# Spacing the routing scatters of two stages over their turns, with four row buffers and loops of four turns

## What is computed

```python
x = x + L0_gnn(layernorm(x), adj)      # 17-tap convolution, messages, GRU gates
x = x + L0_ffn(layernorm(x))           # top 2 of 16 experts
...
# inside the last feed-forward layer
x = x + y @ wo.T                       # causal attention of 4 heads
flat = rmsnorm(x, ln2)
probs = softmax(flat @ router_w.T); tp, ti = top_k(probs, 2)
return x + sum_e weight_e * expert_e(flat)
```

## Time and profile before

| | |
|---|---|
| median of 3 runs | 3343.19 us (3338.99 to 3350.63) |
| the profiled execution | 3378.2 us |
| its span, first to last instruction | 3376.4 us |
| mean granted TensorE clock over the span | 0.904 |
| busy share of the span: PE, PEld, DVE, ACT, POOL | 80%, 63%, 65%, 52%, 26% |
| scatters of routed rows (line 756) | 320, 315.9 us busy |

### The profile page before, as it was taken

The page is one execution under the profiler, slowest core; times in us unless marked ns, Lnnn a source line. Parts: engine busy times, 40 slices in busy tenths (PEclk is TensorE's granted clock), DMA queues, the critical chain, the costliest instruction groups (busy, mean ns, idle before and its releaser), DMA issues. The chain is left out here.

```text
span 3376.4 us, 67489 instructions
## 1 busy us (share of the span) xinstructions
PE 2714.6 (80%) x19706; PEld 2131.5 (63%) x19706; DVE 2205.6 (65%) x6555; ACT 1742.1 (52%) x5034; POOL 872.7 (26%) x863
## 2 busy tenths in 40 slices
PE   5798995888677586578999998899987777669992
PEld 4566674877457585265777877566654444468882
DVE  5666664444467554767888885699986667644445
ACT  2233332444456453475656563677756666445553
POOL 0222332444425343230001010000001343434332
PEclk9899997999789798889999999899998888779996
DMA  5111111222332121320000000000010000022115
GB/s 195 42 46 48 57 45 47 67 63 65 117 123 76 50 58 47 126 79 1 1 1 0 0 1 10 26 19 25 19 34 37 21 24 20 26 59 56 53 53 165
DMA packets 142589, 169.06 MB, mean 50 GB/s; under 512 B 19920, under 2 KB 118224, under 8 KB 141776
## 3 DMA queue, kind: packets, MB, share of 16 engines
q1 hardware_dynamic: 116688, 118.67, 11.9%
q0 software_dynamic: 21504, 44.74, 3.9%
q10 hardware_dynamic: 4224, 3.59, 0.4%
HBM read 115.87 MB, written 51.05 MB: 49 GB/s over the span
## 5 line engine op out<-in xcount | busy, mean ns | idle before, releaser
L1375 PE MATMUL bank<-ffn_e_xT,ffn_e_mine 128*128 128x128 f32 x3360 | 462.8, 285 | 56.3 <-ACT ffn_e_mine L1309 24.4
L1233 POOL DMA_INDIRECT y_rows<-ffn_e_rows_out,ffn_e_scatter_at x352 | 339.0, 963 | 523.4 <-DVE ffn_e_rows_out L1261 331.6
L1375 PEld LDWEIGHTS bank<-ffn_e_xT,ffn_e_mine 128*128 128x128 f32 x3360 | 423.1, 199 | 68.0 <-issue 41.7
L756 POOL DMA_INDIRECT sorted_rows<-ffn_rows,ffn_slot x320 | 315.9, 987 | 231.2 <-issue 220.1
L1385 PE MATMUL bank<-ffn_e_mine,ffn_e_hid 128*128 128x128 f32 x1968 | 294.9, 283 | 39.1 <-DVE ffn_e_hid L1281 17.6
L1281 DVE TENSOR_TENSOR ffn_e_hid<-ffn_e_act,bank 128x256 f32<-128x256 f32 (+1 forms) x280 | 135.9, 485 | 276.3 <-ACT ffn_e_act L1335 245.1
L1309 ACT ACTIVATE ffn_e_mine<-constants 128x512 f32 (+1 forms) x352 | 250.9, 714 | 87.1 <-issue 64.4
L1385 PEld LDWEIGHTS bank<-ffn_e_mine,ffn_e_hid 128*128 128x128 f32 x1968 | 256.2, 196 | 55.9 <-DVE ffn_e_hid L1281 26.5
L2752 ACT ACTIVATE gnn_prob<-bank,gnn_low 128x256 f32<-128x256 f32 x512 | 203.0, 500 | 107.0 <-DVE gnn_low L2666 107.0
L1335 ACT ACTIVATE ffn_e_act<-bank 128x256 f32<-128x256 f32 (+1 forms) x280 | 120.8, 431 | 247.0 <-PE bank L1375 174.1
L1269 DVE TENSOR_SCALAR ffn_e_mine<-constants 128x256 f32 (+2 forms) x352 | 123.6, 354 | 119.6 <-PE bank L1385 73.0
(11 more groups left out here) (515 smaller groups left out, 6552.1 us busy)
## 6 DMA issues: line engine op xcount, KB each, us to landing
g_adj<-in_adjT SPq DMA_DIRECT2D x48, 512.0 KB, 3.8
ffn_e_rows_in<-sorted_rows SPq DMA_DIRECT2D x346, 66.0 KB
ffn_c_y<-y_rows SPq DMA_DIRECT2D x80, 256.0 KB, 3.7
g_adj_rows<-in_adj SPq DMA_DIRECT2D x16, 512.0 KB
gnn_adj<-in_adjT SPq DMA_DIRECT2D x16, 512.0 KB, 3.8
constants<-in_ffn SPq DMA_DIRECT2D x1, 6281.0 KB, 22.1
y_rows<-ffn_e_rows_out,ffn_e_scatter_at POOLq DMA_INDIRECT x352
constants<-in_ffn SPq DMA_DIRECT2D x1, 5204.0 KB, 15.5
```

What stands on the lines that cost most here:

```text
L756: eng.indirect_dma_start(c.sorted_rows, bass.IndirectOffsetOnAxis(r.slot[par][:, k, j:j + 1], 0), r.rows[par][:, j, :], None).then_inc(r.d ...
L1233: g.indirect_dma_start(c.y_rows, bass.IndirectOffsetOnAxis(scatter_at[par][:, k:k + 1], 0), rows_out[par][:, k, :], None).then_inc(scatter ...
L1375: ins = pe.matmul(chunk(part, ch), chunk(weights[:, i * HALF:(i + 1) * HALF], ch), x, start=True, stop=True)
```

## The change

1. **Scatters in eight pieces.** `dispatch` takes a set `mine` of the eight scatters. The new `Route.pool_few` issues those. Ahead of each piece it waits for its own last addition (`paced`) and adds one column of a scratch tile.
2. **gnn0.** GpSimd's turn t scatters the rows of t-2 one at a time, each after a semaphore of TensorE of the same turn. Three of them stand ahead of the root of t-1, which was first before.
3. **att3.** GpSimd's turn t computes the root and the addition first, as before, then scatters 6 and 7 of turn t-3 and 0 to 5 of turn t-2, each (but the first of a group) after one of ScalarE's exponentials.
4. **Buffers.** `ROUTE_DEPTH` is 4 for ffn0 and ffn3; every route call gets a buffer number modulo 4.
5. **Loops.** gnn0 uses `by_fours`: turns 0 to 3 written out, 4 to 11 in a loop of four bodies, 12 to 15 written out. att3 uses the new `staggered_fours` with `STAGES = (2, 3, 8, 4)`: -2 to 7 written out, 8 to 11 in a loop that runs once, 12 to 18 written out.
6. Two semaphores that only ffn1 uses are no longer made for the others, and the last scatters of gnn0 (turn 14 after the loop, turn 15 in the table stage) stay in one piece.

```diff
+def staggered_fours(eng, body, ahead, behind, begin, left):
+    for t in range(-ahead, begin):
+        body(t, t % 4)
+    with eng.Fori(begin, TURNS - left - 3, 4) as t:
+        for i in range(4):
+            body(t + i, i)
+    for t in range(TURNS - left, TURNS + behind):
+        body(t, t % 4)
...
-                def turn(t, par, first, last):
+                def turn(t, four, first, last):
+                    par, one, two = four % 2, (four + 3) % 4, (four + 2) % 4
                     if first:
                         return
+                    if isinstance(t, int) and t == 1:
+                        g.wait_ge(route.zeroed, 2)
+                        route.pool_rstd(g, 0)
+                        return
+                    route.pool_few(g, t - 2, two, (0,))
+                    g.wait_ge(ghn_ps, t + 1)
+                    route.pool_few(g, t - 2, two, (1,))
+                    g.wait_ge(dist_ps, t + 1)
+                    route.pool_few(g, t - 2, two, (2,))
                     route.pool_rstd(g, t - 1)
-                    if not (isinstance(t, int) and t == 1):
-                        route.pool_dispatch(g, t - 2, par)
-                every_turn(g, turn)
+                    g.wait_ge(c2_ps, t + 1)
+                    route.pool_few(g, t - 2, two, (3,))
+                    g.wait_ge(nmp_ps, t + 1)
+                    route.pool_few(g, t - 2, two, (4,))
+                    g.wait_ge(route.logits_ps, t)
+                    route.pool_few(g, t - 2, two, (5,))
+                    g.wait_ge(r_ps, t + 1)
+                    route.pool_few(g, t - 2, two, (6,))
+                    g.wait_ge(z_ps, t + 1)
+                    route.pool_few(g, t - 2, two, (7,))
+                by_fours(g, turn)
                 route.pool_rstd(g, TURNS - 1)
-                route.pool_dispatch(g, TURNS - 2, 0)
+                route.pool_dispatch(g, TURNS - 2, 2)
...
-ROUTE_DEPTH = {"ffn0": 2, "ffn1": 4, "ffn3": 2}
+ROUTE_DEPTH = {"ffn0": 4, "ffn1": 4, "ffn3": 4}
...
-def dispatch(eng, c, m, r, par):
+def dispatch(eng, c, m, r, par, mine=range(2 * TT)):
     for k in range(m.top):
         for j in range(TT):
+            if k * TT + j not in mine:
+                continue
...
+    def pool_few(self, g, t, par, mine):
+        if 0 in mine:
+            done = counted(g, t + 1)
+            g.wait_ge(self.slots_ready, done)
+            g.wait_ge(self.h_ready, done)
+        wait_past(g, self.paced, 2 * TT * t + mine[0])
+        g.tensor_tensor(self.c.tick[:, 5:6], self.c.tick[:, 0:1], self.c.tick[:, 0:1], ALU.add).then_inc(self.paced, 1)
+        dispatch(g, self.c, self.m, self.r, par, mine)
...
-    STAGES = (2, 3, 6, 4)
+    STAGES = (2, 3, 8, 4)
...
                     if on(t - 1):
                         route.pool_rstd(g, t - 1)
                         with_x1(t - 1)
+                    if on(t - 3) and not (isinstance(t, int) and t - 3 == TURNS - 1):
+                        route.pool_few(g, t - 3, (four + 1) % 4, (6,))
+                        after(g, exp_ready, t + 1, 8, 5)
+                        route.pool_few(g, t - 3, (four + 1) % 4, (7,))
                     if on(t - 2) and not (isinstance(t, int) and t - 2 == TURNS - 1):
-                        route.pool_dispatch(g, t - 2, par)
-                staggered(g, turn, *STAGES)
+                        if isinstance(t, int) and t == 2:
+                            g.wait_ge(route.zeroed, 2)
+                        route.pool_few(g, t - 2, (four + 2) % 4, (0,))
+                        for first, turns, exps in ((1, 1, 6), (2, 1, 8), (3, 2, 1), (4, 2, 3), (5, 2, 4)):
+                            after(g, exp_ready, t + turns, 8, exps)
+                            route.pool_few(g, t - 2, (four + 2) % 4, (first,))
+                staggered_fours(g, turn, *STAGES)
```

More of the change, by code:

```diff
@@ L460, in turn @@
                     if not first:
-                        route.vector_shift(v, t - 1, 1 - par, before)
+                        route.vector_shift(v, t - 1, one, before)
                     if not last:
@@ L477, in turn @@
                     if not first:
-                        route.vector_first(v, t - 1, 1 - par, before)
+                        route.vector_first(v, t - 1, one, before)
                         route.vector_second(v, t - 1, before)
@@ L547, in turn @@
                     if not first:
-                        route.scalar_rows(a, t - 1, 1 - par)
+                        route.scalar_rows(a, t - 1, one)
                     a.wait_ge(shared_ps, t + 1)
@@ L643, in turn @@
                     if not first:
-                        route.tensor_hT(pe, t - 1, 1 - par)
+                        route.tensor_hT(pe, t - 1, one)
                     if not last:
@@ L807, in __init__ @@
              "den_ready pair_sum pair_eps pair_inv rank_ps counted used_ready "
-             "picked slots_ready inside_ready kept_ready routed").split())
-        self.scattered = r.dispatched
+             "picked slots_ready routed").split())
+        self.inside_ready, self.kept_ready = (sem(n) if m.capacity else None for n in ("inside_ready", "kept_ready"))
+        self.scattered, self.paced = r.dispatched, sem("paced") if m.top > 1 else None
     def tiles_(self, ap):
@@ L3002, in with_x1, with turn @@
                     g.tensor_tensor(c.X[:, rows_, :], c.X[:, rows_, :], c.X1[:, rows_, :], ALU.add)
-                def turn(t, par):
+                def turn(t, four):
+                    par = four % 2
                     if on(t - 1):
@@ L3124, in turn @@
                         row_stats(t - 1)
-                staggered(v, turn, *STAGES)
+                staggered_fours(v, turn, *STAGES)
             @block.scalar
@@ L3205, in turn @@
                     if on(t - 2):
-                        route.scalar_rows(a, t - 2, par)
+                        route.scalar_rows(a, t - 2, (four + 2) % 4)
                     if on(t - 1):
@@ L3224, in turn @@
                         evac_T(1, 1)
-                staggered(a, turn, *STAGES)
+                staggered_fours(a, turn, *STAGES)
             @block.tensor
@@ L3339, in turn @@
                     if on(t - 2):
-                        route.tensor_hT(pe, t - 2, par)
+                        route.tensor_hT(pe, t - 2, (four + 2) % 4)
                     if on(t - 1):
```

30 lines of the change are left out of this document (15 added, 15 removed).

## The result

The changed kernel takes **3230.05 us** (median of four runs, 3227.11 to 3233.31) beside 3344.07 for the kernel before: a ratio of **0.9658**, 95% interval 0.9639 to 0.9678, or 114 us less. The forecast was 73 us less, 3270, and its range ended at 3230. The direction and both places were right; the size of one place was wrong by a factor of more than two, and a term that I had put at nothing is not nothing.

The account below looks back on a forecast made before the run. Bursts of scatters were taken to hold TensorE's news and so lengthen turns of the graph and attention stages. Spacing them saves 36 + 37 = 73 us from the 3343.2 us median, giving 3270 us, range 3230 to 3325.

Parts of the forecast that it names:

- The mechanism: Graph and attention stages: scatters following each other without a gap hold back news of TensorE's finished matmuls from waiting engines.
- rival B: Only one of the two stages gains, gaps being too short in the attention: 3290 to 3330 us, chance 0.2.
- D: Every single scatter holds TensorE's news for 2.77 us, so the kernel gets slower: 3396 us, chance 0.09.
- From about the second scatter: Where in a burst of scatters the holding of TensorE's news was said to begin.
- Until 2 to 3 us after the last: When the holding was said to end, counted from the start of a burst's last scatter.
- Rival C: Scatters are not the cause, only the norm's delay is added: 3354 us, or 3343 if hidden; chance 0.07.
- Graph stage, 36 us: Turns fall from 30.3 to 27.7 us (26.4 + 0.8 norm's delay + 0.5 residual holds), saving 2.6 in 14 turns.
- The holding is no product of the profiler as a whole: Both stages: 54 + 65 us charged to holding exceed the 35 us by which the profiled execution exceeded the median.
- Attention, 37 us: Spaced scatters leave 22.5 us of the 25.6 us turn, saving 3.1 us in each of twelve turns.
- 2.3 us: Attention: holding left per turn after spacing, about half of an upper bound of 4.2 us.
- 20.2: Attention: undisturbed turn in us, 18.73 plus VectorE's 1.07 of routing and some gaps.
- Loops by four and buffers: Both stages: no gain or loss, longer code covered by prefetch; if that failed, about 1 us per turn.

Follow-up runs that it names:

- e1: Changed kernel with the attention's scatters put back as one burst of eight, so only the graph stage is spaced: 3317.4 us, 0.9928 of before.
- e3: Changed kernel with both stages scattering in one burst of eight again, four buffers and loops by four kept: 3353.0 us, 1.0036 of before.
- e2: Changed kernel with the graph stage's scatters put back as one burst of eight, so only the attention is spaced: 3267.9 us, 0.9776 of before.
- e7: Changed kernel with all eight scatters at the old place, no waits for marks, three chained additions ahead of each: 3260.6 us, 0.9682 of before.
- e8: Changed kernel with scatters in back-to-back pairs, marks between pairs, norm first in the graph stage: 3243.1 us, 0.9636 of before.
- e5: Changed kernel with GpSimd's norm ahead of the three scatters in the graph stage, nothing else: 3246.7 us, 0.9649 of before.
- e11: Changed kernel with the graph stage back to loops by two and two row buffers, scatters still spaced: 3074.4 us, 1.0001 of before (chip C).
- e13: The kernel before, unchanged, run and profiled a second time, on chip D: 3344.1 us, ratio 1.0011.
- e17: Changed kernel with pairs everywhere, graph stage with two buffers, loops by two, norm first; two additions ahead of each experts pair: 3228.1 us, 0.9586 of before.
- e18: Same as e17 but three additions ahead of each pair in the experts stages: 3128.9 us, 0.9297 of before.

## Why the prediction was right and where it was wrong

**The mechanism**, as far as it says that rows of scatters make the readers of finished matmuls late, was right on four chips of five. The waits named "remote" went from both stages, the marks shown above pass within 0.04 us, e1 to e3 put the gain on the spacing, rival B (only one stage gains) falls with e1 and e2, and D (each scatter holds by itself) with the changed kernel and e7. What it is in the chip that delays the news, no run shows. "From about the second scatter" was too early: a pair holds nothing (e8). "Until 2 to 3 us after the last" was near: 1.94 us in ffn0's experts.

**Rival C** (the scatters are not the cause, 3343 to 3354) is what chip C shows: 0.5% slower. The rule of the Trainium skill that I set beside it, "SBUF — State Buffer", section "Who interferes with whom", says that DMA never contends with a compute engine, and it speaks of the ports of SBUF. What I drew from it, that spacing frees nothing, holds on chip C and not on the others, where the time between a finished matmul and its reader grew by microseconds. My "the trace disagrees" went too far: no run shows that this delay has to do with SBUF's ports. But the loss on chip C is not C's term, the norm's delay: e5 prices that at 0.19 us a turn, and e11 gives the whole loss back by undoing loops and buffers.

**Graph stage, 36 us:** 35.6 measured (e3 to e1), by luck: two errors cancel. The start, 30.3 us a turn, was 0.8 to 1.0 too high (29.5 in e3, 29.3 in e13), since I took one execution's interval as it stood although that execution was 35 us over the median. "The holding is no product of the profiler as a whole" was the step that hid it. The costs added to the 26.4 us of an undisturbed turn, 0.8 for the norm and 0.5 for residual holds, were too high as well: the turn takes 27.0, so both together are at most 0.6, and 0.19 of that is the norm (e5). The tick was 0.20 us in place of 0.3.

**Attention, 37 us:** 85.1 measured. This is the step that failed. Two of its terms were mis-sized. The "2.3 us" of residual holds, "about half" between 0 and 4.2, is 0: no "remote" wait is left and the turns are as short as the one without scatters, although the closest starts are 1.37 us apart and not the 1.6 to 1.8 that I had assumed. The row of the burst did not show what two or three such scatters do. I took the middle between two far ends where the row nearest to a single scatter, the logits that passed within 0.4 us, spoke for zero. And the undisturbed turn, "20.2", is 18.7: I added 1.07 us of VectorE's routing and some gaps to 18.73, but VectorE is busy for 206.19 / 12 = 17.2 of 18.7 us, so this work fits into its idle time. 25.6 - 18.7 = 6.9 us would have given 83. That the clock would rise I had named as a sign, not as a term, yet the bound of 18.73 already had it, being a row at 1.00.

**Loops by four and buffers, "nothing":** 11.8 us lost on chip A, 14.6 on chip C. I had said what failure would look like, 1 us a turn. The loss has about that size, but on chip C most of it lies in another stage, one that runs there at a lower clock; "covered by prefetch" was the reason that I gave for nothing, and no run shows whether it is that which failed.

**The sum:** 36 + 37 = 73 forecast; 35.6 + 85.1 - 11.8 = 109 measured by parts.

## What to carry to other kernels

On a chip that shows late "remote" waits, don't start more than two indirect DMAs of GpSimd directly behind each other while TensorE feeds other engines; leave about 2 us between the start of a pair's second and the next pair, with a few tiny additions if nothing better is at hand. Look at every stage that scatters, not only the one that a change touches: here the untouched experts stages gave about as much again (99 us from e17 to e18). And time such a change on more than one chip, because what it cures may be absent from the next one, where only its costs are left.

## What the runs showed that I had not expected

- Chips differ in the holding: three stages without scatters are as long on chip C as on the others (within 0.1 us of chip D in the two traces compared), while the whole kernel before takes 8 to 9% less on chip C (3074 against 3340 to 3368 us).
- In the experts stages the pause has an edge: 1.60 us between a pair and the next holds, 2.0 holds far less; and three short additions of 0.74 us in all, work that computes nothing, are worth 99 us against two. In the graph stage eight scatters 1.38 us apart held nothing.
- One profiled execution stood 35 us above the timed runs, and a second of the same kernel did not.
- Loops by four with four buffers in one stage came with 5 to 9 us more in another whose code is the same; in the middle of it the clock was 0.90 against 1.00.
